# The running sums of the typed sweeps, held at a fixed place and added by TensorE

## The reference

```python
for l in range(3):
    Q, K, V = typed(x, W_Q[l]), typed(x, W_K[l]), typed(x, W_V[l])   # by node type, 8 heads of 32
    scores = sum(Q[dst] * typed(K[src], W_E[l], edge_type), -1) / sqrt(32) * mu[l].T[edge_type]
    e = exp(scores - segment_max(scores, dst)[dst])
    w = e / (segment_sum(e, dst)[dst] + 1e-10)
    agg = segment_sum(V[src] * w[..., None], dst)
    x = layer_norm(x + agg @ Wo[l] + bo[l]); x = layer_norm(x + mlp(x))
```

## Time and profile before

| | before |
|---|---|
| median of runs | 7554.61 us |
| the profiled execution's own time | 7535.38 us |
| its span | 7533.4 us |
| mean granted TensorE clock | 0.89 of full speed |
| TensorE / VectorE / ScalarE busy in the span | 75% / 69% / 41% |

### The profile page before, as it was taken

One profiled execution on the slowest core, in us unless ns is written; L12 is line 12 of the kernel. 1 busy time (PEld: TensorE's weight loads), 2 busy tenths in 40 slices (PEclk: granted clock), 3 DMA queues, 4 the chain that ended last, 5 costly groups with the idle time before them and its releaser, 6 DMA issues. The chain is left out here.

```text
span 7533.4 us, 127045 instructions
## 1 busy us (share of the span) xinstructions
PE 5665.6 (75%) x27620; PEld 4473.2 (59%) x27621; DVE 5193.9 (69%) x17560; ACT 3052.1 (41%) x10171; POOL 3587.6 (48%) x3779
## 2 busy tenths in 40 slices
PE   2788377768888578848888897887988886667776
PEld 1566266647777356636666785665866665544455
DVE  7665388858888656657999658998669996543313
ACT  0111166636666356625555235554345552100025
POOL 0667276635555167724666006664036661057730
PEclk9999999989999678869999999999999998866678
DMA  1000211132222134436666216665146663023330
GB/s 30 3 3 3 45 51 46 47 51 74 73 72 74 29 92 106 106 57 214 177 175 172 67 68 186 176 178 132 64 123 175 176 175 81 9 70 105 105 61 17
DMA packets 336625, 690.60 MB, mean 92 GB/s; under 512 B 96716, under 2 KB 193926, under 8 KB 336006
## 3 DMA queue, kind: packets, MB, share of 16 engines
q0 software_dynamic: 209536, 581.61, 29.7%
q1 hardware_dynamic: 120320, 103.02, 4.4%
q10 hardware_dynamic: 6406, 2.28, 0.1%
HBM read 605.77 MB, written 80.89 MB: 91 GB/s over the span
## 5 line engine op out<-in xcount | busy, mean ns | idle before, releaser
L1012 PE MATMUL bank<-arena,onehots 128*128 128x264 f32 (+3 forms) x6496 | 1955.9, 432 | 226.2 <-DVE onehots L851 99.6
L973 PE MATMUL bank<-arena,spreads 128*128 x5568 | 1459.4, 370 | 598.0 <-ACT spreads L1026 255.5
L937 POOL DMA_INDIRECT arena<-tab_l,slot_typed x1392 | 1325.9, 953 | 904.7 <-issue 285.6
L1012 PEld LDWEIGHTS bank<-arena,onehots 128*128 128x128 f32 x6496 | 1296.2, 219 | 552.7 <-issue 166.1
L973 PEld LDWEIGHTS bank<-arena,spreads 128*128 128x128 f32 x5568 | 964.7, 205 | 825.9 <-issue 752.4
L937 POOL DMA_INDIRECT arena<-tab_l,slot_src x928 | 886.7, 956 | 482.7 <-issue 255.3
L1205 DVE TENSOR_TENSOR acc<-acc,bank 128x264 f32 (+3 forms) x1624 | 657.1, 405 | 468.6 <-PE bank L1012 459.1
L1026 ACT ACTIVATE spreads<-bank 128x256 f32<-128x256 f32 x1392 | 524.4, 377 | 905.9 <-PE bank L961 903.6
L1100 DVE TENSOR_TENSOR arena<-arena,bank 128x512 f32<-128x512 f32 x928 | 631.1, 681 | 232.1 <-ACT stats L1048 137.0
L937 POOL DMA_INDIRECT arena<-tab_l0b,slot_src x464 | 444.8, 959 | 479.7 <-ACT arena L1066 253.0
L860 ACT ACTIVATE onehots<-iota_row,slot_loc 128x128 f32<-128x128 f32 x1856 | 632.6, 391 | 17.5 <-PEq L1861 8.3
(11 more groups left out here) (360 smaller groups left out, 9535.9 us busy)
## 6 DMA issues: line engine op xcount, KB each, us to landing
tab_l<-arena SPq DMA_DIRECT2D x150, 384.0 KB, 3.1
arena<-tab_l,slot_typed POOLq DMA_INDIRECT x1392
arena<-tab_l,slot_src POOLq DMA_INDIRECT x928
arena<-tab_l0a,slot_src POOLq DMA_INDIRECT x464
arena<-tab_l0b,slot_src POOLq DMA_INDIRECT x464
rec_dram<-arena POOLq DMA_INDIRECT x417, 2.1
arena<-L_gnn_w SPq DMA_DIRECT2D x6, 1024.0 KB, 10.0
tab_l<-arena SPq DMA_DIRECT2D x25, 132.0 KB, 1.7
```

The source lines that it names most:

```text
L937: pool.indirect_dma_start(out=rows_sb[:, a, t, 0:width], out_offset=None, in_=table[:, :], in_offset=bass.IndirectOffsetOnAxis(ap=index[:, ...
L973: mm = pe.matmul(z[x.k % 2][:, t, 0:cw], spreads[:, x.k % 2, t * P:t * P + P], qtab[:, block_no[w], 0:cw], start=True, stop=not gatv2)
L1012: mm = pe.matmul(sums[x.k % 2], onehots[:, x.a, GT * x.k + t, :], rhs, start=t == 0, stop=t == GT - 1)
```

## The change

The typed sweeps no longer let VectorE add. `current`, a fixed piece of SBUF (`att[:, 0:wc]`), holds the sums of the block that is being summed. TensorE adds it to the group's sums by one more product with the identity matrix onto the same PSUM bank. ScalarE then copies the bank twice: to `current`, scaled by 1 or 0 from the new table `goes_on` (1 where the next group has the same node block), and to the block's rows in `acc`. The rescaling of a batch acts on `current`, one slot earlier (LAG "add_up", 15), and TensorE waits for it in the first group of a batch. ScalarE loads the block numbers, VectorE does not. `tile_border` becomes bfloat16.

```diff
-        tile_border = sb("tile_border", [P, NB * 33])
+        tile_border = sb("tile_border", [P, NB * 33], BF16)
+        goes_on = sb("goes_on", [P, NB * BG])
...
+                    link(dve.memset(goes_on[:, :], 0.0))
+                    link(dve.tensor_tensor(goes_on[:, 1:GRP], block_f[:, 1:GRP], block_f[:, 0:GRP - 1], ALU.is_equal))
...
+            current = att[:, 0:wc]
...
-                                               start=t == 0, stop=t == GT - 1)
+                                               start=t == 0, stop=t == GT - 1 and not hgt)
+                            if hgt:
+                                if needed(x.g):
+                                    pe.wait_ge(S["added_up"].sem, S["added_up"].at(x.g))
+                                if x.k == 0:
+                                    pe.wait_ge(S["rescaled"].sem, S["rescaled"].at(x.batch + 1))
+                                mm = pe.matmul(sums[x.k % 2], ident[:, :], current, start=False, stop=True)
                             mm.then_inc(S["summed"].sem, 1)
...
                     def slot_fn(i, w):
+                        nonlocal block_no
+                        if hgt and w == 0 and not (isinstance(i, int) and G16 * i < LAG["keep"]):
+                            block_no = next_blocks(mybir.EngineType.Activation, 0, G16 * i - LAG["keep"], G16)
+                        x = Group(i, w, LAG["keep"])
+                        if x.there and hgt:
+                            act.wait_ge(S["summed"].sem, S["summed"].at(x.g + 1))
+                            if not (isinstance(i, int) and x.g == NB * BG - 1):
+                                act.activation(current, sums[x.k % 2], ACT.Copy, scale=goes_on[:, ds(x.g + 1, 1)])
+                            act.activation(acc[:, block_no[w], 0:wc], sums[x.k % 2], ACT.Copy)\
+                               .then_inc(S["added_up"].sem, 1)
...
-                        x = Group(i, w, LAG["keep"])
-                        if x.there:
+                        x = Group(i, w, LAG["add_up"] if hgt else LAG["keep"])
+                        if x.there and not (hgt and x.k > 0):
                             if needed(x.g):
                                 dve.wait_ge(S["added_up"].sem, S["added_up"].at(x.g))
-                            av = acc[:, block_no[x.k if gin else w], 0:wc]
+                            av = current if hgt else acc[:, block_no[x.k if gin else w], 0:wc]
...
+                        if x.there and not hgt:
                             dve.wait_ge(S["summed"].sem, S["summed"].at(x.g + 1))
                             dve.tensor_tensor(av, av, sums[x.k % 2], ALU.add).then_inc(S["added_up"].sem, 1)
```

More of the change, by code:

```diff
@@ L1019, in _ @@
                 def _(act):
+                    block_no = None
                     def slot_fn(i, w):
+                        nonlocal block_no
[8 more added lines that the diff above has]
+                               .then_inc(S["added_up"].sem, 1)
                         x = Group(i, w, LAG["turn"])
@@ L1089, in _ @@
                     dve.memset(seg_max[:, :, :], 0.0).then_inc(step.sem, 1)
+                    if hgt:
+                        dve.memset(current, 0.0)
                     dve.wait_ge(step.sem, step.at(2))
@@ L1188, in slot_fn @@
                             dve.tensor_reduce(r, lane_split(pr, C), AX, ALU.add).then_inc(S["raw_made"].sem, 1)
-                        if w % (BG if gin else G16) == 0 and not (isinstance(i, int) and G16 * i + w < LAG["keep"]):
+                        if w % (BG if gin else G16) == 0 and not hgt and not (isinstance(i, int) and G16 * i + w < LAG["keep"]):
                             block_no = next_blocks(mybir.EngineType.DVE, 0, G16 * i + w - LAG["keep"], BG if gin else G16)
-                        x = Group(i, w, LAG["keep"])
-                        if x.there:
+                        x = Group(i, w, LAG["add_up"] if hgt else LAG["keep"])
+                        if x.there and not (hgt and x.k > 0):
                             if needed(x.g):
                                 dve.wait_ge(S["added_up"].sem, S["added_up"].at(x.g))
-                            av = acc[:, block_no[x.k if gin else w], 0:wc]
+                            av = current if hgt else acc[:, block_no[x.k if gin else w], 0:wc]
                             if x.k == 0 and not gin:
```

## The result

The changed kernel takes 7644.8 us (median of five runs, 7640.56 to 7721.45) against 7554.61, 90 us or 1.2% more. The ratio on record, 1.0143 with a 95% interval of 1.011 to 1.0177, goes by all runs, the longest too, and so lies above the ratio of the medians. Slower, as forecast; 7670 had been named.

A forecast was written before the change was run, and what follows sets the result against it. VectorE narrowly paces the plain slots; the change moves that bound to TensorE. Stretches sum to +1.96 us, 24.43 at full clock; with 0.63 for the clock 25.06, +115 us over 87 batches, 7670 us, range 7530 to 7780.

The forecast's parts named there:

- VectorE's relief: The addition leaves VectorE, 2.7 us a batch, 237 us in all; on the path only where TensorE waits for VectorE.
- A plain slot of 2.42 us: TensorE's slot grows from 1.97 us by the identity product's 0.445, passing VectorE's earlier 2.14; the bound moves to TensorE.
- The wait ahead of L954 pays for most of the products here: Slot 0 to L954: TensorE's products mostly fill its existing wait, so the mean rises only 0.14 us, 7.85 to 7.99.
- Slot 6 to slot 0: TensorE waits in slot 7 for VectorE's rescaling: 5.94 us against 3.95, a loss of 1.99, of which 1.10 is wait.
- Slot 0: From here to L954, three plain slots take 7.26 us, 1.46 more with the register load; mean 7.99 at full clock.
- L954 to slot 4: TensorE's stretch before the next slot 4, 2.31 us before, grows by the product's 0.445.
- slots 4 to 6: TensorE's stretch from slot 4 to slot 6: 7.74 us against 8.36 at full clock, a gain of 0.62.
- Low clock 0.63 us a batch: TensorE's clock falls behind slot 5's waits; half the present price of 1.27 us was taken, between nothing and 1.56.
- Rival A: Product fits TensorE's idle time and VectorE's relief counts: batch 22.6 us, -99 us, 7455 us; chance 15%.
- B: No change: rescaling is ready in time for slot 7 and the clock costs 0.4: 7555 us; chance 8%.
- D: ScalarE becomes the pace: copies at 0.39 delay one-hots, another 1.0 us a batch, 7757 us; chance 10%.
- C: Clearly slower: clock falls as often as now because slot 7's new wait adds idle time: 25.99 us, 7750 us; chance 17%.

The follow-up runs named there:

- e1: Changed kernel, but VectorE rescales an unused piece and TensorE doesn't wait for it; the product stays: 7533.86 us, 1.0007 to the kernel before.
- e3: Kernel before plus TensorE's identity product on a zeroed piece, no new wait, VectorE adding as before: 7554.99 us, 1.0007 to the kernel before.
- e2: Changed kernel without the identity product, its two waits kept ahead of the last segment product: 7576.19 us, 1.0033 to the kernel before.
- e4: Changed kernel without ScalarE's second copy, that to the block's rows: 7610.43 us, 1.0095 to the kernel before.
- e9: Kernel before with ScalarE's powers copy first in slot 6 and TensorE's register load split 5 and 11: 0.9929 to the kernel before, on a slower chip.
- e12: Changed kernel with ScalarE's powers copy first in slot 6 and TensorE's register load split 5 and 11: 1.0018 to the kernel before, on a slower chip.

## Why the prediction held, step by step

- VectorE's relief, 2.7 us a batch, of little use: right. The chain between the two L973 stayed at 4.10 and the way to L998 shortened from 2.04 to 1.67 (1.68 forecast). e1 has product and relief without the wait, e3 the product without the relief, and both take as long as the kernel before.
- A plain slot of 2.42 us, product 0.445: right. Slots 1 and 2 are 2.47 and 2.46.
- "The wait ahead of L954 pays for most of the products here": right, and truer than I made it. In e3 the waits in slots 2 and 4 and the clock pay for all of them.
- Slot 6 to slot 0 at 5.94, of which 1.10 is wait: right in its steps (VectorE's weighting 2.45 us after slot 6 began, forecast 2.41; the rescaling 2.40 later, forecast 2.48; TensorE's product 0.57 after it, forecast 0.60). The batch shown is a short one with 5.95; the mean is 6.13, slot 7 being 1.26 over a plain slot.
- Slot 0: right without the clock, wrong with it. Three slots to L954 were to be 7.99 us and are 3.70 + 2.47 + 2.46 = 8.63. Where the clock stays up slot 0 is 3.89 with the load and 2.42 without, 3.15 on the mean, and the three make 8.08. The rest are the falls that the wait in slot 7 and the register load bring together. I had looked for falls only behind slot 5. L954 to slot 4 was to be 2.76 and is 2.53; slots 4 to 6 were 7.74 without the clock and are 8.00 with it.
- Low clock 0.63 us a batch, half of before: the size came, the mechanism did not. Half as many falls behind slot 5 had been assumed; there they went from 51 batches to 7, and 32 new ones in slot 0, 1.6 us each, cost the 0.6 us. That the two agree is luck. The sum of 24.43 and the measured 25.1 to 25.3 leave 0.7 to 0.9 for the clock and all other errors. A clock of 0.96 to 0.97 was named and came.
- The total has luck in it too: the typed sweeps lost 130 us by the profile where 115 had been forecast, and the 16 us of the sweeps ahead of them, in no sum, bring it back.
- What the prediction had wrong is the weight of the parts. By its list each of several terms gives some loss, and they add. By e1 taking the wait out brings back 1.4 of 1.5 us a batch, by e3 the product alone costs nothing, and by e2 the wait alone costs 0.5: the parts do not add. One reason it states itself for slots 4 and 5: work that fills a wait is free. It did not apply it to the clock, where the product takes falls away behind slot 5.
- Rival A (the product goes into idle time, and VectorE's relief counts) holds in its first half: e3 shows the room. Its second half falls, and not only for the new wait: e1 has the relief and no such wait, and a batch takes 23.75 us, not 22.6. The rule of the Trainium skill, Perfetto Trace Analysis, "Identifying the Most-Contended Engine", fares the same: it saw room on TensorE (weight loads 62%), and e3 used it free of charge; VectorE, of the highest occupancy, was relieved from 91 to 77%, and nothing was gained. What the Trainium skill, TensorE: Matmul & The Clock Gate, "Why this matters for your kernels", says on idle gaps agrees with e3, whose filled gaps go with 0.98 instead of 0.94, and with the falls of slot 0 behind two idle stretches. B is out by the 3.68 us of slot 7, D by e4 and plain slots of 2.42 to 2.47. C had a true part, falls of the clock that the wait in slot 7 brings, but not its size: 39 batches with falls against 51 before, and 25.2 us instead of 25.99.

## What to carry to other kernels

When work is handed from the busiest engine to two others, look at the order inside the slot of the one that gets it: whatever now stands behind the new work is late, and the engine that was relieved may be the one that waits for it. Before a per-batch step is moved one slot ahead, follow its inputs back through every engine; here one copy of 0.26 us stood behind 2 us of other work, and moving it to the front took back the 1.9% that the change cost on that chip, and won 0.7 to 0.8% in the kernel before too. Take such a change apart into its product and its wait and run each alone, and both together; the sums of a walk do not say which of them matters, since the parts fill each other's gaps. And look at what stands next to a new wait: a second idle stretch right behind it, here a register load of 1.1 us, can bring the clock down where neither does so alone.

## What the runs showed of the hardware

- The clock fell behind two idle stretches of TensorE close together (0.9 us, three instructions, 1.1 us) in slot 0 of 32 of 42 batches, and behind either of them alone in none: not in e1, where the load stands alone, and not in the changed kernel's batches without a load.
- TensorE's sequencer loads 16 block numbers in 1.11 us, 5 in 0.59 and 11 in 2.65 (e9, e12). Whether the count or the odd place of the first number in the table makes the last one long was not tried.
- ScalarE's copy with a scale from a table (L1040, 128x264) takes 0.48 us and delays the next one by 0.37 (4703.26 to 4703.63), while the plain copy of the same size (L1041) delays by 0.27. I had taken 0.29 for both.
- Adding work to TensorE can cost nothing for a second reason beside filled waits: in e3 it is busy for 55 us more in a sweep of 665 and its clock rises from 0.94 to 0.98.
- The same kernel takes 7552 us on one chip and 8964 to 9037 us on another, with the same durations of instructions and gaps that are released by "remote". What it is was not tried.
